# Four attentions: the normalisation one slot later in VectorE's order, the next value projection ahead of the first weighing in TensorE's

## The reference

```
x = x + jnp.tanh(g_xattn[2]) * attn(_layernorm(x), ctx_1024, ctx_1024, ...)

def attn(q, k, v, mask, w_q, w_k, w_v, w_o):
    Q, K, V = (proj(q, w_q), proj(k, w_k), proj(v, w_v))     # (B, 16 heads, S=64, 8)
    scores = einsum('bhqd,bhkd->bhqk', Q, K) / sqrt(8)
    scores = where(keep, scores, NEG)
    attn = softmax(scores, axis=-1)
    x = einsum('bhqk,bhkd->bhqd', attn, V)
    return x.transpose(0, 2, 1, 3).reshape(B, -1, 128) @ w_o.T
```

## Time and profile before

| | |
|---|---|
| Median of 3 runs | 3282.54 us (3276.01 to 3284.56) |
| Profiled execution, its own time | 3298.21 us |
| Its span, first to last instruction | 3296.4 us |
| TensorE busy | 2532.8 us, 77% |
| VectorE, ScalarE, GpSimd busy | 1566.6, 1380.2, 978.3 us |
| Mean granted TensorE clock | 0.886 of full |

### The profile page before, as it was taken

One profiled execution on the slowest core, in us unless ns is written; L12 is line 12 of the kernel. 1 busy time (PEld: TensorE's weight loads), 2 busy tenths in 40 slices (PEclk: granted clock), 3 DMA queues, 4 the chain that ended last, 5 costly groups with the idle time before them and its releaser, 6 DMA issues. The chain is left out here.

```text
span 3296.4 us, 74894 instructions
## 1 busy us (share of the span) xinstructions
PE 2532.8 (77%) x28202; PEld 1794.6 (54%) x28202; DVE 1566.6 (48%) x4283; ACT 1380.2 (42%) x1992; POOL 978.3 (30%) x1052
## 2 busy tenths in 40 slices
PE   4888864439997799989999969993288777358883
PEld 2555543328886455567777735551145444247773
DVE  3555544424443577622222247776667665513322
ACT  2555533213332466644545436661055444124441
POOL 4444426634444112110000000001112433634444
PEclk9999976669999899989999979996599888679997
DMA  3010101126665222100000011110011111146666
GB/s 98 22 24 20 23 16 38 39 80 195 197 192 153 78 53 61 34 3 0 0 0 0 1 44 45 41 41 11 11 32 31 37 35 37 44 144 191 189 186 219
DMA packets 143775, 219.56 MB, mean 67 GB/s; under 512 B 27177, under 2 KB 94513, under 8 KB 143026
## 3 DMA queue, kind: packets, MB, share of 16 engines
q1 hardware_dynamic: 96930, 90.25, 10.8%
q10 hardware_dynamic: 29232, 90.37, 8.8%
q0 software_dynamic: 17408, 36.21, 3.2%
HBM read 157.48 MB, written 43.61 MB: 61 GB/s over the span
## 5 line engine op out<-in xcount | busy, mean ns | idle before, releaser
L1541 DVE TENSOR_REDUCE mx<-psS 128x16 f32<-128x1024 f32 x264 | 322.6, 1222 | 321.9 <-PE psS L1096 294.1
L650 POOL DMA_INDIRECT yg<-ysb,yidx x288 | 279.5, 970 | 421.0 <-DVE ysb L2005 190.6
L470 POOL TENSOR_TENSOR ve<-mv,eps 128x4 f32<-128x4 f32 x102 | 20.3, 199 | 1184.4 <-DVE mv L1517 1182.3
L756 ACT ACTIVATE work<-psT 128x1024 f32<-128x1024 f32 x260 | 266.2, 1024 | 215.5 <-PE psT L1105 214.8
L750 ACT ACTIVATE work<-work 128x1024 f32<-128x1024 f32 x264 | 278.3, 1054 | 135.9 <-DVE work L1543 132.7
L1096 PE MATMUL psS<-kexp,qT 64*64 64x512 f32 x2112 | 307.6, 634 | 31.0 <-DMA kexp<-kT 15.3
L1543 DVE TENSOR_TENSOR work<-psS,mx 128x1024 f32<-128x1024 f32 x264 | 323.2, 1224 | 9.1
L1105 PEld LDWEIGHTS psT<-ident,work 128*128 128x128 f32 x2080 | 239.6, 145 | 151.5 <-issue 99.8
L1105 PE MATMUL psT<-ident,work 128*128 128x128 f32 x2080 | 288.3, 283 | 5.3 <-ACT work L756 3.3
L1381 PEld LDWEIGHTS psY<-w_ffn,work 128*128 128x128 f32 x2016 | 247.8, 192 | 9.4 <-DVE work L1976 1.2
L1381 PE MATMUL psY<-w_ffn,work 128*128 128x128 f32 x2016 | 248.5, 275 | 1.6 <-DVE ysb L1999 1.0
(11 more groups left out here) (278 smaller groups left out, 4645.0 us busy)
## 6 DMA issues: line engine op xcount, KB each, us to landing
w_ffn<-in_wmoe ACTq DMA_DIRECT2D x72, 578.0 KB
w_ffn<-in_wmoe ACTq DMA_DIRECT2D x72, 576.0 KB
ctxT<-in_ctxT SPq DMA_DIRECT2D x76, 256.0 KB, 2.8
xin<-xg SPq DMA_DIRECT2D x144, 132.0 KB
kexp<-kT SPq DMA_DIRECT2D x1152, 16.0 KB
gio<-yg SPq DMA_DIRECT2D x16, 512.0 KB, 3.9
work<-yg SPq DMA_DIRECT2D x16, 512.0 KB, 6.4
yg<-ysb,yidx POOLq DMA_INDIRECT x288
```

Source lines behind the costliest of these rows:

```text
L650: e.indirect_dma_start(out=yg, out_offset=bass.IndirectOffsetOnAxis(ap=yidx[:, b, t:t + 1], axis=0), in_=ysb[:, b, t, :], in_offset=None, ...
L756: e.activation(pT[:, s % 2, :], psT[:, :], ACT.Copy).then_inc(pt_ok, 1)
L1541: e.tensor_reduce(mx[:, :], src, AX, ALU.max).then_inc(s_max, 1)
```

## The change

On VectorE `normalise` of chunk u no longer stands at the end of turn u but in slot 0 of turn u+1, behind `shift` of tile 2 and ahead of `combine` (attention 1) and `x_update`. The last chunk's stands behind the last turn. On TensorE `v_proj` of chunk u+1 in slot 0 stands ahead of `weigh` of tile 0 rather than behind it. No instruction is added or removed, and no wait of an instruction is changed.

```diff
@@ TensorE, attention, turn @@
                         p_turn(lay, i, *ahead(u, s, 1))
-                        weigh(lay, i, u, s)
                         if s == 0:
                             v_proj(lay, i, u + 1)
+                        weigh(lay, i, u, s)
@@ TensorE, attention_routed @@
+                        if s == 0 and inside:
+                            v_proj(lay, None, u + 1)
                         if inside:
                             weigh(lay, None, u, s)
-                        if s == 0 and inside:
-                            v_proj(lay, None, u + 1)
@@ VectorE, attention, turn @@
                         shift(lay, i, *ahead(u, s, 2))
                         if s == 0:
+                            if i is not None or u >= 1:
+                                normalise(lay, i, u - 1)
                             if lay == 1 and u + 2 < CHUNKS:
                                 combine(i, u + 2)
...
-                    normalise(lay, i, u)
...
                 turn(None, CHUNKS - 1)
+                normalise(lay, None, CHUNKS - 1)
@@ VectorE, attention_routed @@
                             shift(lay, None, *ahead(u, s, 2))
                         if s == 0:
+                            if 1 <= u <= CHUNKS:
+                                normalise(lay, None, u - 1)
                             if 2 <= u < CHUNKS + 2:
                                 x_update(lay, None, u - 2)
...
-                    if inside:
-                        normalise(lay, None, u)
```

## The result

The changed kernel takes 3287.61 us (median of 20 runs, 3282.66 to 3291.33) against 3280.7 us for the kernel before (20 runs on the same chip, 3273.41 to 3287.39). The ratio is 1.0023, with a 95% interval of 1.0015 to 1.003: a loss of 5 to 10 us that lies inside what the prediction called no measurable change. The forecast was 3286.6 us, 4.1 us more than the kernel before; 6.9 us more were measured. That the two times lie only 1.0 us apart comes in part from the kernel before, whose median fell from 3282.54 us to 3280.7 with more runs. The number fits better than the reasons do, as the rest of the text shows.

The account below looks back on a forecast made before the run. TensorE's own order was taken to set the pace in attentions 1 and 2. Terms +1.0, +1.5, -1.0, -2.0 and +4.6 sum to +4.1 us, giving 3286.6 us on the median's scale (3282.5), with an 8-in-10 range of 3269 to 3304.

Parts of the forecast that it names:

- The path through slot 0: From the end of tile 2's scores through reduction, subtraction, normalisation and release to tile 0's weighing: 3.25 us, weighing then 1.02.
- the -0.07 of the sum: Attention 2: the query projection starts at 2094.59 against 2094.66, -0.07 us a turn, -1.0 us in all.
- 1195.00 + 3.25 = 1198.25 for the weighing: Attention 1, slot 0: start of the weighing; the query projection follows at 1200.47 against 1200.37, +0.10 us a turn, +1.5 in 15.
- It is hidden: Attention 1: tile 3's reduction comes about 1.1 us later, covered because the exponential behind it waits for ScalarE's copy of tile 2.
- In these turns +0.17 vanishes in that wait: Attention 0: the +0.17 us a turn disappears in 9 turns that wait 1.4 us each for key copies; other 6 give +1.0.
- the 0.17 of the sum: Attention 0: second value pass, then weighing, put tile 3's scores at 380.80 against 380.63, +0.17 us a turn.
- a rival of attentions 1 and 2: TensorE's clock falls behind one idle piece of about 1.2 us; about 11 us lost in each, time about 3309; chance 0.08.
- 0.65 us each in the first, third and fourth of them: Attention 3, turns without a scatter: -0.65 us in turns 1, 3 and 4, 0 in turns 2, 5 and 6, -2.0 in all.
- If the scatter sets that end, the whole 1.14 us comes through: Attention 3: tile 3's reduction is 1.14 us later, delaying the scatter; turns 8, 10, 12, 14 give +4.6, odd turns 0.
- the marks that I set: Expected signs: windows of attentions 0, 1 and 2 within 3 us of 357.6, 282.0 and 283.3; attention 3 loses in even turns from 8.
- a sign that the prediction is wrong: Attention 3: odd turns moving by more than 0.5 us would show the prediction wrong.

Follow-up runs that it names:

- The experiment with the wait: Both moves in attention 1 alone, GpSimd's addition of expert results made to wait for the layer norm, against the kernel before: 3210.65 us against 3213.91, ratio 0.9989.
- the second comparison: The changed kernel run once more, unaltered, on another chip against the kernel before: 3216.26 us against 3213.91, ratio 0.9999 (0.9985 to 1.0014).

## Why the prediction held, and where its steps did not

**The path through slot 0 (3.25 us, then the weighing) was right.** Measured are 3.30 us. In attention 2 the turn went from 18.86 to 18.79 us, the -0.07 of the sum.

**Attention 1: right mechanism, a missing term.** The step read "1195.00 + 3.25 = 1198.25 for the weighing", and +0.10 us a turn. The experiment with the wait leaves just 0.10. On top came 0.24 us of VectorE's tensor_scalar behind GpSimd, so 0.345 x 15 = +5.2 us instead of +1.5. I had followed the lateness of the reduction of tile 3 ("It is hidden") as far as ScalarE, and not on to the statistics and what GpSimd does with them.

**Attention 0: the step that failed.** It was "In these turns +0.17 vanishes in that wait", with 9 turns counted as covered and the clock taken as it was. The wait for ScalarE's copy grew to 2.07 to 2.18 us, and the weighing and the scores behind it run at the low clock in every turn of the loop. In the later turns that is 0.85 us for the weighing and up to 0.73 for the scores, with the 0.17 of the sum 1.75 us, where the wait for the key copies had 1.1 to 1.4 to give. What is left over is 0.35 to 0.65 us a turn; the last six turns take 23.86 us on average instead of 23.40. In all it is +4.4 us in 13 turns, where +1.0 was counted. I had made the clock a rival of attentions 1 and 2, where it stayed at 1.00, and not of attention 0, whose longest piece of idle time the change lengthens. I had also read that piece in one turn, 1.79 us; in other turns of the kernel before it is up to 2.20 us. The Trainium skill, TensorE: Matmul & The Clock Gate, section "HAM oscillation — how this bites in real kernels", describes a kernel whose clock falls each time its bursts of matmuls are parted by a wait. Here the trace agrees behind 2.07 us, and shows none behind 1.20.

**Attention 3, early turns: the size was right, its place not.** The six turns give -2.1 us against -2.0. They are 17.32, 18.68, 18.55, 19.94, 19.94 and 22.12 us after 18.75, 18.74, 18.76, 20.56, 20.56 and 21.26: one turn gives 1.43 us, two 0.62 us each, and the last takes 0.86 back. The sum had 0.65 us each in the first, third and fourth of them and nothing in the others, so that the total agrees is luck.

**Attention 3, turns with a scatter: "If the scatter sets that end, the whole 1.14 us comes through" failed in its second half.** From the end of the scores of tile 2 to the first scatter of the turn it was 15.11 us (2662.22 - 2647.11) and is 16.22 us in the changed kernel (2658.60 - 2642.38), so the 1.1 us do reach the scatter. They don't last. By the same ends, from this scatter to the odd turn's scores it is 14.09 us instead of 14.19, from there to the odd turn's scatter 13.31 instead of 13.77, and from that to the next even turn's scores 16.24 instead of 18.19. Two turns are thus 1.40 us shorter in this pair of executions, not 1.14 longer. TensorE's rows of the changed kernel from the scatter on show what such a turn waits for:

```profile
2659.58 0.89 PE L1125 MATMUL psY<-work,ones 128*32 128x128 f32 x10
2660.76 0.38 PE L1125 MATMUL psY<-work,ones 128*32 128x128 f32 x3 [0.29 <-issue]
2661.52 0.33 PE L1125 MATMUL psY<-work,ones 128*32 128x128 f32 x2 [0.38 <-issue]
2662.29 0.27 PE L1125 MATMUL psY<-work,ones 128*32 128x128 f32 x1 [0.44 <-issue]
2663.02 0.49 PE L1146 MATMUL psX<-w_att,aT 128*128 128x128 f32 x3 [0.46 <-issue]
...
2670.01 2.68 PE L1096 MATMUL psS<-kexp,qT 64*64 64x512 f32 x5 [0.56 <-issue]
```

The 16 matmuls of one weighing come as ten, three, two and one, and each later piece follows idle time in which TensorE waited for nothing that the profile shows. In this turn it starts just behind the first scatter and goes on some 4 us behind the last (issued at 2667.67). In the other chips' executions the 9 turns take some 65 us less, and a weighing beside the same eight transfers often comes whole; the kernel with attention 1 alone has one at 2600.85 with all 16 in 0.62 us, amid transfers from 2595.09 to 2604.18. The orders are no longer told apart there. On the first chip each of the nine turns is 0.3 to 1.1 us shorter, 5.4 us together. That this belongs to the change is not shown: it is one execution of each kernel, that of the kernel before (3298.21 us) is 10.8 us longer than the longest of its 20 timed runs, and the kernel with only these turns changed speaks against it.

**The sum.** The terms from the turns are +4.4, +5.2, -0.9, -2.1 and about 0, so +6.6 us, against +6.9 us measured; the forecast had +1.0, +1.5, -1.0, -2.0 and +4.6. The zero is taken from the other chips. With the 5.4 us that the nine turns lost on the first chip it would be +1.2, and on the chip of the second comparison +6.6 us lies above the interval, so the agreement is not proof. What the forecast owes to luck is plain all the same: a term too high in the scatters' turns stood in for two too low in attentions 0 and 1. Of the marks that I set, the windows of attentions 0 and 1 kept within 3 us, that of attention 2 (280.28 us) lies a hair outside; the even turns of attention 3 didn't lose, and the odd ones moved by 0.5 to 1.1 us (one from 30.68 to 29.59 us), which I had named as a sign that the prediction is wrong. For attention 3 it was. Open remain why the changed kernel's loss is 0.0023 on one chip and none on another (the terms make 0.002 on both), and the 6 us by which the timed gain of attention 3's early turns exceeds what its turns show.

## What to carry to other kernels

An instruction that fills another wait is not free to move: look at what it filled, and ask what that idle piece becomes, since behind a longer one the clock may fall for everything that follows. When an engine is made late by a microsecond, follow it to the engine it feeds as well as the one it waits for, and look which instructions now run side by side. And judge a change in repeated turns turn by turn; here the turns were steady to 0.1 us while whole executions of one kernel differed by 10 us and more.

## What the runs showed of the hardware

- **A tensor_scalar behind GpSimd.** The 128x128 tensor_scalar from SBUF to SBUF takes some 0.34 us alone. Where GpSimd's 128x512 addition starts 0.25 us ahead of the first of four, that one takes 1.12 us and ends with the addition; the others take 0.33. In the same turns VectorE's reductions (1.22 us, from PSUM) did not change.
- **The clock behind a wait.** Behind waits of 0.81 and 1.20 us it never fell in attentions 1 and 2. In attention 0 before, with waits of 1.74 to 2.20 us, it fell in some turns; in the changed kernel, with 2.07 to 2.18 us, in every turn from the third on. With the normalisation alone, behind 2.19 to 2.28 us in attentions 1 and 2, it fell in about every third. The length of the wait alone doesn't decide: with the weighing between the passes it fell behind a wait of 1.90 us for the key copies and not behind one of 2.17. At the low level one weighing holds TensorE for 1.87 us (380.34 to 382.21) instead of 1.02.
- **Turns with scatters differ by chip.** The same nine turns of the unchanged order took 276.14 us on the first chip and 208.6 to 212.7 us on the three others, where whole runs take 3213 to 3215 us instead of 3281. On the first chip TensorE's matmuls start in pieces of one to five while GpSimd issues its indirect transfers; on the others they often come whole. What holds them up is not shown. A candidate that no run tested is the supply of instructions: the turns with scatters are written out, and the profile's instruction queue of the changed kernel moved 26 packets from 2500 to 2790 us and 1 from 200 to 400 us, in attention 0's loop.
